# Attention tile: key and query factor spread over the outer products in place of the values, two product pairs summed on GpSimd

## The chip, the cores and the metric

The kernel runs on one core of a Trainium2 chip. The metric is the device time in microseconds of one execution, lower being better. Each time is that of a whole launch, so that constant loads at the start and the last store at the end count. In what follows PE is TensorE, DVE is VectorE, ACT is ScalarE, POOL is GpSimd and SP is SyncE, which here only issues DMAs.

## The reference, cut to what matters

All arithmetic is float32. The input is 4 sequences of 1024 tokens with 128 features. An attention layer, a feed-forward layer and a mixture with eight low-rank experts follow each other. The change is in the attention, with H = 16 heads of DH = 8 columns:

```
q = sigmoid(x @ Wq + bq); k = sigmoid(x @ Wk + bk); v = x @ Wv + bv
... (two rounds of running sums give sink_in, sink_alloc and src_comp, a factor per token and head)
qs = q * (sink_in / normal)[..., None]
vs = v * src_comp[..., None]
kv = jnp.cumsum(jnp.einsum('bhld,bhlm->bhldm', k, vs), axis=2)
x = jnp.einsum('bhld,bhldm->bhlm', qs, kv) * sink_alloc[..., None]
attn = x @ Wo + bo
```

For each token and head there is an outer product of 8 key columns d with 8 value columns m. It is summed along the tokens, and then contracted over d with the query factor. The projection by Wo follows.

## The kernel before, in words

The 4096 tokens are cut into 8 tiles of 512. A tile is held with the 128 features on the partitions (head times 8 plus column) and its tokens along the free axis. Odd tiles carry on the running sums of the even tile before them.

The instruction order of each engine is written out by hand. After an `opening` for tile 0 and a `second_step`, the function `step(s)` runs once per tile and works on four tiles at once: `a` = s+1 is in its attention denominators, `b` = s in its outer products, its output projection and its feed-forward layer, `c` = s-1 in the gate and the first half of the experts, `d` = s-2 in the second half of the experts. `closing` drains the last tiles. An engine takes its instructions strictly in this order. A wait on a semaphore holds all that stands behind it on the same engine, SP's queue of DMAs included.

The outer products go by value column m, in eight rounds:

1. `spread_vs(t, m)` on SP (L292) copies row m of each head of `vs` onto all 8 partitions of the head, from SBUF to SBUF, into `vb[:, m, :]`. It needs `vs`, which `values` (L1032) makes on DVE.
2. `outer_product(t, m)` on DVE (L1037) is `kv = k * vb[m]`: partition (h, d) holds column d of the key times value column m.
3. `cumulate_kv(t, m)` on DVE (L1043) is the running sum along the tokens. The first scan operand is a bank of ones in PSUM.
4. `product(t, m)` on POOL (L848) is `prod = cum_kv[m] * q_fac`. `prod` has four slots.
5. `reduce_out(t, m)` on PE (L404) multiplies the product, 128 tokens at a time, by `s_wor[:, m, :]`, a matrix in which row m of each head of Wo is repeated over the 8 partitions of the head. It sums over d and projects at once, in four matmuls (eight instruction records) of 128x128, into the PSUM bank `pO`.

The rounds 0 to 3 of tile `a` are begun at the end of a step, and the rounds 4 to 7 run at the beginning of the next step, where the tile has become `b`. `moments(b, 0)` on DVE waits for all eight `reduce_out`, and `inverse_std(b, 0)` on POOL for the moments.

The neighbours that the prediction speaks of are these. On POOL: `scaled_n2` (L874), `outer_residual` (L879), `inverse_std` (L835 to L841, four small instructions), `shifted_x` (L858), `constant_residual` (L886, writes `x2c`). On DVE: `second_relu` (L1141), `cumulate_q` and `cumulate_k` (L937), `k_times_cum_q` (L957, writes `kq`), `q_times_cum_k` (L964, writes `qk`). On PE: `expert_out` (L508), `project_v` (L340), and `head_sums` (L354), which takes `kq` and then `qk` and from which the denominators of the next tile come; further `hidden` (L421), `ffn_out` (L428), and `constant_row` (L517), done once, whose result `r_cmoe` DVE finishes.

## Time and profile before

| what | value |
|---|---|
| median of 3 runs | 418.44 us (418.27 to 419.03) |
| the profiled execution | 418.39 us, span 416.6 us |
| PE busy | 374.6 us, 90% |
| DVE busy | 327.9 us, 79% |
| POOL busy | 223.2 us, 54% |
| ACT busy | 216.6 us, 52% |
| DMA queue of SP | 25.96 MB, 24.5% of 16 engines |
| one step in the middle | 44.4 to 44.7 us |

The span goes from the first to the last instruction of the profiled execution. Its own time is 1.8 us longer. Busy times are those of the profile, and several engines work at the same time, so that they do not add up to the span.

### The profile page before, as it was taken

The numbers are of one execution on the slowest core, as the hardware profiler recorded it, in microseconds if no ns is written. First come the engines' busy times: TensorE is split into PE (matmuls) and PEld (weight loads), VectorE is DVE, ScalarE is ACT, GpSimd is POOL, SyncE is SP. The second block draws the span as 40 slices with busy tenths as digits, with TensorE's granted clock in tenths as the row PEclk, the third lists the DMA queues.
The fourth block names the chain that finished last, engine by engine and source line by source line (L and its number), as shares of the span: only waits on it lengthen the run. The fifth ranks groups of instructions, "written<-read, shape, count | busy, mean of one in ns | idle before, by whom it ended". The sixth has DMA issues, their size and how long they took to land.

```text
span 416.6 us, 6454 instructions
## 1 busy us (share of the span) xinstructions
PE 374.6 (90%) x2082; PEld 261.3 (63%) x2082; DVE 327.9 (79%) x787; ACT 216.6 (52%) x399; POOL 223.2 (54%) x263
## 2 busy tenths in 40 slices
PE   8897789788998999989998999899989997799991
PEld 3555556465756875677657774778478765775551
DVE  3649966599589988999799979997899889832632
ACT  2240226327853586538852795278644874175541
POOL 2017234983279527963497348942795369735211
PEclk9999999899999999999999999999999999999997
DMA  8236006400180007300560028000810063000000
GB/s 257 115 71 158 1 2 152 125 3 0 37 217 2 0 2 183 97 0 2 116 162 2 0 56 223 3 0 16 204 36 0 2 160 68 0 1 27 12 14 25
DMA packets 19857, 26.58 MB, mean 64 GB/s; under 512 B 1648, under 2 KB 9968, under 8 KB 19824
## 3 DMA queue, kind: packets, MB, share of 16 engines
q1 hardware_dynamic: 19680, 25.96, 24.5%
q8 instruction: 17, 0.28, 0.3%
q10 hardware_dynamic: 144, 0.21, 0.3%
q14 instruction: 16, 0.13, 0.1%
HBM read 7.29 MB, written 2.10 MB: 23 GB/s over the span
## 4 chain that ended last, share of the span: by engine, by line
PE 31%; DVE 27%; POOL 19%; issue 14%; DMA 5%; ACT 2%; SPq 0%; POOLq 0%; DVEq 0%; ACTq 0%
POOL prod L848 12%; PE pB L354 5%; DMA vb<-vs 5%; DVE kv L1037 5%; PE pY L428 4%; PE pG L421 3%; DVE cum_kv L1043 3%; DVE cum_ks L937 2%; PE pG L497 2%; POOL rstd L838 2%; PE pG L490 2%; DVE cum_q L937 2%; PE pY L508 2%; DVE cum_qs L937 2%; DVE gel L1141 2%
## 5 line engine op out<-in xcount | busy, mean ns | idle before, releaser
L848 POOL TENSOR_TENSOR prod<-cum_kv,q_fac 128x512 f32<-128x512 f32 x64 | 94.5, 1483 | 33.9 <-DVE cum_kv L1043 25.7
L404 PEld LDWEIGHTS pO<-s_wor,prod 128*128 128x128 f32 x512 | 62.2, 191 | 33.5 <-POOL prod L848 21.4
L404 PE MATMUL pO<-s_wor,prod 128*128 128x128 f32 x512 | 69.5, 281 | 14.0 <-POOL prod L848 13.9
L1037 DVE TENSOR_TENSOR kv<-k,vb 128x512 f32<-128x512 f32 x64 | 52.8, 825 | 6.7 <-DMA vb<-vs 6.7
L835 POOL TENSOR_TENSOR var_eps<-mv,s_con 128x4 f32<-128x4 f32 x32 | 9.9, 310 | 71.1 <-DVE mv L1063 71.1
L1043 DVE TENSOR_TENSOR_SCAN cum_kv<-p_ones,cum_kv,kv 128x512 f32<-128x512 f32 x32 | 40.5, 1275 | 0.6
L1043 DVE TENSOR_TENSOR_SCAN cum_kv<-p_ones,kv 128x512 f32<-128x512 f32 x32 | 38.5, 1213 | 0.5
L657 ACT ACTIVATE v<-pA,s_att 128x512 f32<-128x512 f32 x7 | 4.8, 687 | 62.9 <-PE pA L340 62.9
L754 ACT ACTIVATE relu<-pG,s_att 128x512 f32<-128x512 f32 x28 | 19.2, 684 | 27.4 <-PE pG L490 27.4
L508 PEld LDWEIGHTS pY<-s_moe,gel 128*128 128x128 f32 x256 | 30.7, 192 | 3.7 <-issue 1.9
L508 PE MATMUL pY<-s_moe,gel 128*128 128x128 f32 x256 | 32.6, 276 | 0.0
L838 POOL TENSOR_TENSOR rstd<-var_eps,s_con 128x4 f32<-128x4 f32 x32 | 32.5, 1014 | 0.0
L428 PE MATMUL pY<-s_ffn,gel 128*128 128x128 f32 x256 | 32.3, 276 | 0.0
L428 PEld LDWEIGHTS pY<-s_ffn,gel 128*128 128x128 f32 x256 | 30.4, 192 | 1.0 <-ACT pY L723 0.5
L421 PE MATMUL pG<-hT,s_ffn 128*128 128x512 f32 x64 | 30.5, 598 | 0.2
L484 PE MATMUL pG<-x2T,s_moe 128*128 128x512 f32 x60 | 30.6, 594 | 0.0
L490 PE MATMUL pG<-u1T,s_moe 128*128 128x512 f32 x60 | 30.5, 592 | 0.0
L497 PE MATMUL pG<-udT,s_moe 128*128 128x512 f32 x60 | 29.5, 605 | 0.0
L1141 DVE SCALAR_TENSOR_TENSOR gel<-pG,neg_bi,relu 128x512 f32<-128x512 f32 x28 | 20.3, 744 | 10.6 <-PE pG L497 10.5
L891 POOL TENSOR_TENSOR e_norm<-esrc,s_con 128x64 f32<-128x64 f32 x8 | 2.8, 346 | 40.8 <-ACT esrc L684 40.8
L354 PEld LDWEIGHTS pB<-s_att,kq 128*128 128x128 f32 x128 | 16.0, 191 | 12.5 <-issue 9.6
L712 ACT ACTIVATE gel<-pG,s_att 128x512 f32<-128x512 f32 x32 | 21.9, 685 | 2.8 <-PE pG L421 2.5
(164 smaller groups left out, 772.7 us busy)
## 6 DMA issues: line engine op xcount, KB each, us to landing
vb<-vs SPq DMA_DIRECT2D x64, 256.0 KB, 4.7
xT<-x_t SPq DMA_DIRECT2D x8, 256.0 KB, 4.3
xt<-x SPq DMA_DIRECT2D x8, 256.0 KB, 5.3
out<-y SPq DMA_DIRECT2D x8, 256.0 KB, 2.3
s_moe<-moe_w SPq DMA_DIRECT2D x1, 836.0 KB, 10.4
s_wor<-wo_rep SPq DMA_DIRECT2D x1, 512.0 KB, 8.2
s_ffn<-ffn_w SPq DMA_DIRECT2D x1, 512.0 KB, 8.9
s_con<-consts SPq DMA_DIRECT2D x1, 502.0 KB, 4.4
```

Source lines behind the costliest of these rows:

```text
L354: mm = pe.matmul(pB[:, end - P:end], src[:, s * P:(s + 1) * P], wide_sum, start=True, stop=True)
L404: mm = pe.matmul(pO3[:, s, :], prod[:, m % 4, s * P:(s + 1) * P], s_wor[:, m, :], start=False, stop=(m == DH - 1), skip_group_check=True)
L421: pe.matmul(pG[f % 2][:, :], w1[:, f * P:(f + 1) * P], hT[:, :], start=True, stop=True).then_inc(w1_done, 1)
L428: mm = pe.matmul(pY3[:, s, :], gel[:, f, s * P:(s + 1) * P], w2[:, f, :], start=False, stop=(f == FC - 1), skip_group_check=True)
L484: pe.matmul(expert_bank(t, f)[:, :], moe("wi")[:, f * P:(f + 1) * P], x2T[t.par][:, :], start=True, stop=False)
L490: pe.matmul(expert_bank(t, f)[:, :], moe("lb")[:, f * P:(f + 1) * P], u1T[:, :], start=False, stop=True).then_inc(in1_done, 1)
L497: pe.matmul(expert_bank(t, f)[:, :], moe("lb")[:, f * P:(f + 1) * P], udT[:, :], start=False, stop=True, skip_group_check=True).then_inc(i ...
L508: mm = pe.matmul(pY3[:, s, :], hsum[:, f, s * P:(s + 1) * P], wo[:, f, :], start=(f == 0 and s == 0), stop=(f == FC - 1), skip_group_check ...
L838: pool.tensor_tensor(rstd[i][:, :], var_eps[i][:, :], con("mhalf"), ALU.pow).then_inc(rstd_ready[i], 1)
L848: pool.tensor_tensor(prod[:, m % 4, :], cum_kv[t.par][:, m, :], q_fac[t.par][:, :], ALU.mult).then_inc(prod_ready, 1)
L1037: dve.tensor_tensor(kv[:, m % 3, :], k[t.par][:, :], vb[:, m, :], ALU.mult).then_inc(kv_ready, 1)
L1043: dve.tensor_tensor_scan(cum_kv[t.par][:, m, :], scan_ones, kv[:, m % 3, :], start, ALU.mult, ALU.add).then_inc(cumkv_ready, 1)
```

## The change

The outer products go by key column d instead of by value column m. Partition (h, m) now holds value column m, so that `vs` is used as it is. Row d of each head of `k` is spread by DMA into a ring of four slots `kb` (`spread_k`), and row d of each head of `q_fac` into `qb[:, d, :]` (`spread_q`). That makes 16 spreads of 256 KB a tile in place of 8. A product of one d is then a partial sum of the same output x, so that products can be added to each other before the projection, and all use the same Wo (`s_wo`, 64 KB in place of 512 KB). POOL adds products 0 and 1, and products 2 and 3 (`pair_sum`), so that PE does six `reduce_out` a tile in place of eight.

The orders change as well: the `reduce_out` of round 0 moves from the end of a step into the next, `expert_out(d, 0)` comes ahead of the later `reduce_out`, `factor_T` comes one `ffn_out` earlier, `query_factor` and the first round come ahead of `moments(b, 1)`, and `constant_row` moves from `opening` into `second_step`.

```
+PAIRS = 2
+SUMS = DH - PAIRS
...
-            def spread_vs(t, m):
-                sp.wait_ge(vs_ready, t.n + 1)
-                src = vs[m:P:DH, :].unsqueeze(1).to_broadcast([HEADS, DH, TOK])
-                sp.dma_start(vb[:, m, :], src).then_inc(vb_loaded[m], 16)
+            def spread_k(t, i):
+                sp.wait_ge(k_ready, t.n + 1)
+                wait(sp, kv_ready, DH * t.n + i - 3)
+                src = k[t.par][i:P:DH, :].unsqueeze(1).to_broadcast([HEADS, DH, TOK])
+                sp.dma_start(kb[:, i % 4, :], src).then_inc(kb_loaded[i], 16)
+            def spread_q(t, i):
+                sp.wait_ge(qfac_ready, t.n + 1)
+                wait(sp, prod_ready, DH * (t.n - 1) + i + 1)
+                src = q_fac[t.par][i:P:DH, :].unsqueeze(1).to_broadcast([HEADS, DH, TOK])
+                sp.dma_start(qb[:, i, :], src).then_inc(qb_loaded[i], 16)
...
-            sp.dma_start(s_wor[:, :, :], wo_rep).then_inc(y_free[0], 16)
+            sp.dma_start(s_wo[:, :], wo_att).then_inc(y_free[0], 16)
+            for i in range(4):
+                spread_k(Tile(0), i)
...
-                if B: spread_vs(b, 4); spread_vs(b, 5); spread_vs(b, 6)
                 if A and a.n == 2: load_xT(a)
+                if B: spread_k(b, 6); spread_k(b, 7)
+                if A and a.n >= 1:
+                    for i in range(4):
+                        spread_k(a, i)
                 if A and a.n >= 1: load_xt(a)
-                if B: spread_vs(b, 7)
                 if A and a.plus(1).exists() and a.n >= 2: load_xT(a.plus(1))
-                if A: spread_vs(a, 0); spread_vs(a, 1)
+                if A:
+                    for i in range(4):
+                        spread_q(a, i)
+                    spread_k(a, 4)
                 if D: store(d)
-                if A: spread_vs(a, 2); spread_vs(a, 3)
+                if A:
+                    for i in range(4, DH):
+                        spread_q(a, i)
+                    spread_k(a, 5)
...
+                if r < PAIRS:
+                    pe.wait_ge(pair_ready, PAIRS * t.n + r + 1)
+                    m = 2 * r
+                else:
+                    m = r + PAIRS
+                    pe.wait_ge(prod_ready, DH * t.n + m + 1)
...
-                if B: reduce_out(b, 1)
-                if A: project_k(a)
                 if D: inter2(d, 2); inter2(d, 3)
-                if B: reduce_out(b, 2)
+                if B: reduce_out(b, 0)
...
-                if B: reduce_out(b, 3); reduce_out(b, 4)
+                if D: expert_out(d, 0)
+                if B: reduce_out(b, 1)
                 if C: logits(c)
-                if B: reduce_out(b, 5); reduce_out(b, 6); reduce_out(b, 7)
-                if D: expert_out(d, 0)
+                if B: reduce_out(b, 2); reduce_out(b, 3); reduce_out(b, 4); reduce_out(b, 5)
                 if A: project_v(a); head_sums(a, 0, True); head_sums(a, 0, False)
...
-                if B: ffn_out(b, 2); ffn_out(b, 3)
+                if B: ffn_out(b, 2)
+                if A: factor_T(a)
+                if B: ffn_out(b, 3)
                 if C: u_T(c, False)
-                if A: factor_T(a)
...
-                if A: reduce_out(a, 0)
...
+            def pair_sum(t, r):
+                pool.wait_ge(prod_ready, DH * t.n + 2 * r + 2)
+                pool.tensor_tensor(prod[:, 2 * r, :], prod[:, 2 * r, :], prod[:, 2 * r + 1, :], ALU.add).then_inc(pair_ready, 1)
...
-                if B: product(b, 1); product(b, 2)
+                if B: product(b, 1); pair_sum(b, 0); product(b, 2)
                 if C: inverse_std(c, 2)
-                if B: product(b, 3); product(b, 4); product(b, 5); product(b, 6); product(b, 7); shifted_x(b)
+                if B: product(b, 3); pair_sum(b, 1); product(b, 4); product(b, 5); product(b, 6); product(b, 7); shifted_x(b)
...
-                dve.tensor_tensor(kv[:, m % 3, :], k[t.par][:, :], vb[:, m, :], ALU.mult).then_inc(kv_ready, 1)
+                dve.tensor_tensor(kv[:, m % 3, :], kb[:, m % 4, :], vs[:, :], ALU.mult).then_inc(kv_ready, 1)
...
+                if A: query_factor(a); outer_product(a, 0); cumulate_kv(a, 0)
                 if B: moments(b, 1)
-                if A: query_factor(a); outer_product(a, 0); cumulate_kv(a, 0)
```

In `product` the second factor becomes `qb[:, m, :]`, with a wait for its DMA, and in all waits `DH` on `red_ready` becomes `SUMS`.

## Rows read from the trace of the kernel before

**Rows 1.** The profile's page: granted clock of PE in 40 slices, in tenths.
```profile
PEclk9999999899999999999999999999999999999997
```
**Rows 2.** Busy time in stretches: us, PE, PEld, DVE, ACT, POOL (instructions), clock, DMA share.
```profile
222.90:267.60 44.70, 42.17 (x253) 31.06 (x253) 40.74 (x99) 27.23 (x50) 27.85 (x32) 1.00 0.27 66
...
252.30:272.20 19.90, 18.06 (x102) 12.59 (x102) 19.72 (x30) 6.51 (x12) 17.61 (x15) 1.00 0.35 91
...
238.08:252.33 14.25, 14.25 (x80) 10.07 (x81) 10.91 (x38) 12.08 (x27) 6.18 (x11) 1.00 0.35 81
```
**Rows 3.** Timeline of POOL, one middle step: start us, us, instruction, idle before.
```profile
253.97 1.60 POOL L879 TENSOR_TENSOR res<-res,x_b2n 128x512 f32<-128x512 f32 x1
255.71 3.05 POOL L848 TENSOR_TENSOR prod<-cum_kv,q_fac 128x512 f32<-128x512 f32 x2
258.72 0.65 POOL L835 TENSOR_TENSOR var_eps<-mv,s_con 128x4 f32<-128x4 f32 x1
...
267.80 1.27 POOL L848 TENSOR_TENSOR prod<-cum_kv,q_fac 128x512 f32<-128x512 f32 x1 [0.27 <-DVE cum_kv L1043]
...
270.25 1.27 POOL L886 TENSOR_TENSOR x2c<-x,c_gate 128x512 f32<-128x512 f32 x1
```
**Rows 4.** Timeline of DVE, the same step.
```profile
248.20 0.69 DVE L1037 TENSOR_TENSOR kv<-k,vb 128x512 f32<-128x512 f32 x1 [0.20 <-DMA vb<-vs]
...
253.00 1.43 DVE L1037 TENSOR_TENSOR kv<-k,vb 128x512 f32<-128x512 f32 x1
...
265.74 0.67 DVE L1037 TENSOR_TENSOR kv<-k,vb 128x512 f32<-128x512 f32 x1
...
271.17 0.91 DVE L957 SCALAR_TENSOR_TENSOR kq<-k,cum_q 128x512 f32<-128x512 f32 x1
...
272.10 0.67 DVE L964 SCALAR_TENSOR_TENSOR qk<-q,cum_k 128x512 f32<-128x512 f32 x1
```
**Rows 5.** Timeline of PE where a step meets the next one's denominators.
```profile
269.12 1.16 PE L404 MATMUL pO<-s_wor,prod 128*128 128x128 f32 x8 [0.38 <-POOL prod L848]
270.12 1.06 PE L508 MATMUL pY<-s_moe,gel 128*128 128x128 f32 x8
271.01 1.02 PE L340 MATMUL pA<-xT,s_att 128*128 128x512 f32 x2
272.22 1.13 PE L354 MATMUL pB<-s_att,kq 128*128 128x128 f32 x8 [0.19 <-DVE kq L957]
273.19 1.06 PE L354 MATMUL pB<-s_att,qk 128*128 128x128 f32 x8
```
**Rows 6.** SP's DMA issues in the same step.
```profile
249.31 4.46 SPq L292 DMA_DIRECT2D vb<-vs  x5
```
**Rows 7.** All instructions on tile vb: time of its DMAs to landing.
```profile
DMA to landing us min/median/max: 3.1/4.7/6.3
```
**Rows 8.** DVE and PE timelines of the opening.
```profile
29.46 0.69 DVE L1037 TENSOR_TENSOR kv<-k,vb 128x512 f32<-128x512 f32 x1 [2.69 <-DMA vb<-vs]
...
25.80 1.06 PE L517 MATMUL pM<-s_moe,bi_rep 128*128 128x128 f32 x8
```
**Rows 9.** Timelines of second_step and step 1: DVE, POOL, PE.
```profile
67.37 0.69 DVE L1037 TENSOR_TENSOR kv<-k,vb 128x512 f32<-128x512 f32 x1 [2.61 <-DMA vb<-vs]
...
78.14 1.26 POOL L879 TENSOR_TENSOR res<-res,x_b2n 128x512 f32<-128x512 f32 x1
...
67.85 3.73 PE L428 MATMUL pY<-s_ffn,gel 128*128 128x128 f32 x32
...
76.54 1.17 PE L404 MATMUL pO<-s_wor,prod 128*128 128x128 f32 x8 [2.38 <-POOL prod L848]
...
94.08 1.13 PE L354 MATMUL pB<-s_att,kq 128*128 128x128 f32 x8
```
**Rows 10.** POOL timeline of the last step.
```profile
343.07 1.59 POOL L879 TENSOR_TENSOR res<-res,x_b2n 128x512 f32<-128x512 f32 x1
...
356.89 1.27 POOL L848 TENSOR_TENSOR prod<-cum_kv,q_fac 128x512 f32<-128x512 f32 x1 [0.28 <-DVE cum_kv L1043]
```

More of the change, by code:

```diff
@@ L63, in run_steps, with build @@
         step(Tile(n))
-def build(nc, x, x_t, att_w, consts, wo_rep, rows, gate_row, ffn_w, moe_w, out):
+def build(nc, x, x_t, att_w, consts, wo_att, rows, gate_row, ffn_w, moe_w, out):
     ctx = ExitStack()
@@ L216, in build @@
         xt_loaded = [sem(f"xt_loaded{i}") for i in range(2)]
-        vb_loaded = [sem(f"vb_loaded{m}") for m in range(DH)]
+        kb_loaded = [sem(f"kb_loaded{d}") for d in range(DH)]
+        qb_loaded = [sem(f"qb_loaded{d}") for d in range(DH)]
         y_free = [sem(f"y_free{i}") for i in range(2)]
@@ L239, in build @@
         compT_ready, vs_ready = sem("compT_ready"), sem("vs_ready")
-        kv_ready, cumkv_ready, prod_ready, red_ready = (sem(n) for n in ("kv_ready", "cumkv_ready", "prod_ready", "red_ready"))
+        kv_ready, cumkv_ready, prod_ready, pair_ready, red_ready = (
+            sem(n) for n in ("kv_ready", "cumkv_ready", "prod_ready", "pair_ready", "red_ready"))
         res_ready = [sem(f"res_ready{i}") for i in range(4)]
@@ L396, in compensation_T, with reduce_out @@
                 spread_T(pB, comp_x[:, :, :].rearrange("p a b -> p (a b)"), compT_ready)
[L398 to L400 removed]
+            def reduce_out(t, r):
+                if r == 0:
                     pe.wait_ge(xseed_ready, t.n + 1)
[L402 removed]
+                if r < PAIRS:
[4 more added lines that the diff above has]
+                    pe.wait_ge(prod_ready, DH * t.n + m + 1)
                 for s in range(SUB):
[L404 to L405 removed]
+                    mm = pe.matmul(pO3[:, s, :], prod[:, m % 4, s * P:(s + 1) * P], s_wo[:, :],
+                                   start=False, stop=(r == SUMS - 1), skip_group_check=True)
                 mm.then_inc(red_ready, 1)
@@ L543, in opening @@
                 compensation_T(a); factor_T(a)
-                constant_row()
                 project_q(a.plus(1)); project_k(a.plus(1))
@@ L547, in opening @@
                 pe.wait_ge(y_free[0], 16)
-                reduce_out(a, 0)
             def second_step(b):
@@ L553, in second_step @@
                 keep_busy(2)
-                for m in range(1, 5):
-                    reduce_out(b, m)
+                reduce_out(b, 0); reduce_out(b, 1)
                 head_sums(a, 0, True); head_sums(a, 0, False); project_v(a)
                 keep_busy(1)
-                reduce_out(b, 5)
+                reduce_out(b, 2)
                 denominators_T(a, 0); denominators_T(a, 1)
                 keep_busy(1)
-                reduce_out(b, 6)
+                reduce_out(b, 3)
                 head_sums(a, 1, True)
@@ L565, in second_step @@
                 keep_busy(1)
-                reduce_out(b, 7)
+                reduce_out(b, 4); reduce_out(b, 5)
                 keep_busy(2)
@@ L572, in second_step @@
                     hidden(b, f)
+                constant_row()
                 for f in range(FC):
                     ffn_out(b, f)
-                keep_busy(3, pM)
-                reduce_out(a, 0)
+                keep_busy(3, pG[1])
             def closing(c):
@@ L843, in product @@
             def product(t, m):
-                if m == 0:
-                    pool.wait_ge(qfac_ready, t.n + 1)
+                pool.wait_ge(qb_loaded[m], 16 * (t.n + 1))
                 pool.wait_ge(cumkv_ready, DH * t.n + m + 1)
-                wait(pool, red_ready, DH * t.n + m - 3)
-                pool.tensor_tensor(prod[:, m % 4, :], cum_kv[t.par][:, m, :], q_fac[t.par][:, :], ALU.mult).then_inc(prod_ready, 1)
+                slot = m % 4
+                if m < 4:
+                    wait(pool, red_ready, SUMS * (t.n - 1) + (4 + slot) - PAIRS + 1)
+                elif slot < 2 * PAIRS:
+                    pool.wait_ge(red_ready, SUMS * t.n + slot // 2 + 1)
+                else:
+                    pool.wait_ge(red_ready, SUMS * t.n + slot - PAIRS + 1)
+                pool.tensor_tensor(prod[:, slot, :], cum_kv[t.par][:, m, :], qb[:, m, :], ALU.mult).then_inc(prod_ready, 1)
+            def pair_sum(t, r):
+                pool.wait_ge(prod_ready, DH * t.n + 2 * r + 2)
+                pool.tensor_tensor(prod[:, 2 * r, :], prod[:, 2 * r, :], prod[:, 2 * r + 1, :], ALU.add).then_inc(pair_ready, 1)
             def attention_input(t):
@@ L906, in second_step @@
                 a = b.plus(1)
-                for m in range(1, DH):
+                product(b, 1); pair_sum(b, 0); product(b, 2); product(b, 3); pair_sum(b, 1)
+                for m in range(4, DH):
                     product(b, m)
```

33 lines of the change are left out of this document (15 added, 18 removed).

## The prediction

> **What bounds the kernel now.** I read the table of stretches first, then the chain that ended last, then the timelines of the engines along that chain. A middle step takes 44.7 us and PE is busy for 42.2 of them, which looks like a kernel bound by PE [rows 2]. Two stretches of the step say more. From 238.08 to 252.33 PE is busy for 14.25 of 14.25 us: it runs hidden layers, transposes and expert products without a gap, and DVE waits for it. There is no output projection in this stretch [rows 2]. From 252.30 to 272.20 DVE is busy for 19.72 of 19.90 us and PE for 18.06, so that DVE sets the pace [rows 2]. DVE hands over to PE at 272.22, where `head_sums` has waited 0.19 us for `kq` [rows 5]. PE and DVE thus take turns in setting the step.
>
> A third party stands close behind. POOL makes its last product at 267.80 to 269.07 [rows 3]. PE then does the last `reduce_out` at 269.12, `expert_out(d, 0)` at 270.12, `project_v` at 271.01 and would be free for `head_sums` at 271.01 + 0.86 = 271.87 (its 1.02 us, less the 0.16 us by which each group overlaps the next: 269.12 + 1.16 against 270.12) [rows 5]. So the products could end only 0.35 us later before PE, and not `kq`, set the start at 272.22. POOL's 27.85 busy us of 44.70 [rows 2] hide this: in the stretch 252.30 to 272.20 it is busy for 17.61 of 19.90.
>
> One more thing is to be seen. The `kv` at 253.00 took 1.43 us where the one at 265.74 took 0.67, and it ended at 254.43 [rows 4]. On POOL, L879 was issued at 253.97 and lasted 1.60 us, though `x2c` of the same shape lasted 1.27 [rows 3]. Both engines read two SBUF tensors there, and each is stretched by the time in which the other has the memory. The same holds for `kq` at 271.17, 0.91 us [rows 4], beside `x2c`, which runs until 271.52 [rows 3], and for `var_eps`, 0.65 us [rows 3]. The Trainium skill (SBUF — State Buffer, "Who interferes with whom") says that a DVE instruction with two SBUF inputs and a reading GpSimd instruction exclude each other for the whole of one of them; the durations above agree. It speaks against this change. By this rule POOL's products end later, as summed below; without it, the nine instructions and `inverse_std` behind 255.57 would take 12.85 us and end at 268.4, before the present end.
>
> **The change, part by part.**
>
> *PE.* Two `reduce_out` a tile go, at 269.12 to 270.12 = 1.00 us each [rows 5], so 16 us of PE work in all. None lies in the stretch in which PE sets the pace, and in the other PE has gaps. Moving `expert_out(d, 0)` ahead takes 271.01 - 270.12 = 0.89 us from between the last `reduce_out` and `project_v` [rows 5]. This widens the slack of the last product from 0.35 to 1.24 us.
>
> *POOL.* Two additions of 512 columns a tile are added. An undisturbed POOL instruction of this shape takes 1.27 us, about 1.25 from start to start [rows 3]. They come between the products on which the end depends. I count the time in which DVE's and POOL's reads exclude each other, from the end of L879, 253.97 + 1.60 = 255.57. Before: seven products, 7 x 1.25 = 8.75; `inverse_std(c, 2)`, 1.6 (about 2.05 with its stall of 0.65 - 0.20 = 0.45); five `kv` of 0.6 (0.67 [rows 4] less the overlap with the next) = 3.0. The sum is 13.35, which gives 268.9, against 269.07 measured [rows 3]. So the count holds. After: nine instructions, 11.25, plus 1.6 and 3.0, less up to 0.6 where a `kv` slips under the tiny instructions of `inverse_std`: 15.25 to 15.85, ending at 270.8 to 271.4. I take 271.0. PE: 271.05 + 1.00 + 0.86 = 272.9 for `head_sums`, against 272.22. This is +0.7 us a step if nothing else is disturbed.
>
> *What is queued behind.* `shifted_x` and `x2c` stand behind the last product on POOL. Before, they ran under scans and PSUM reads of DVE and only `kq` met the end of `x2c`. Now they come at 271.0 to 273.5, just when DVE wants `kq` (271.2) and `qk`. If `kq` comes in ahead of `shifted_x`: `kq` to 271.6, `shifted_x` to 272.85, `qk` to 273.45, and the second half of `head_sums`, due at 272.9 + 0.97 = 273.87, does not wait: +0.7 us. If `shifted_x` comes in first: it ends at 272.25, `kq` 272.85, `x2c` 274.1, `qk` 274.7, and the second half starts at 274.75 instead of 273.19 [rows 5]: +1.6 us. Which comes first hangs on a tenth of a microsecond, and on the scans, which are a little longer in odd tiles. I take the middle, +1.2 us a step, and keep +0.7 and +1.6.
>
> *DVE.* It issues as many instructions as before. The wait for the spread of `vs`, 0.20 us in a middle step [rows 4], goes, but it lies before a wait for PE's stretch, so it gives nothing. `query_factor` moves ahead of `moments(b, 1)`; that delays `inverse_std(b, 1)` to about 251.0, just when ACT can use it: nothing.
>
> *Transfers.* Sixteen spreads a tile. SP issues five in 4.46 us, 0.89 each [rows 6], and a spread lands 3.1 to 6.3 us after its issue [rows 7]. `q_fac` is ready at about 246.3. Behind it stand q0 to q3, k4, a store, q4 to q7, k5: k5 is issued at 246.3 + 10 x 0.89 = 255.2 and lands at 258.3 to 261.5. DVE wants it at 261.6. q0 lands at about 249.5, and POOL wants it at 251. All is hidden, the last with little to spare by the upper bound. The spreads of k0 to k3 wait in the queue for the last `kv` of the step before (about 267) and are needed 25 us later. `load_xt` and `load_xT` behind them are late by some 15 us, and needed later still.
>
> *Start.* The first `kv` waits 2.69 us for its spread, the one of tile 1 2.61 us [rows 8, 9]. Both waits go, the second with the 0.6 us of `q_fac` under it. But kb4 of tile 0 stands fifth behind the q spreads and takes back about half of the first gain. Later, `moments(0, 1)` waits for `ffn_out`, which ends at 71.58 [rows 9] and into whose way `constant_row` comes, 1.06 - 0.16 = 0.9 us [rows 8]. With 1.5 us gained ahead of it I get -0.6 us at the end of L879, 79.40 [rows 9], so 78.8. DVE is ahead now and no longer paced by scans, so that four `kv`, `kq` and `qk` all fall among POOL's nine instructions: 78.8 + 11.25 + 1.6 + 1.8 (four `kv`, one under `inverse_std`) + 1.2 = 94.65. PE: + 1.9 = 96.55, against 94.08 [rows 9]. I take +2.4 us through step 1, with +0.7 (if half of the conflicts do not occur and the gain is 2) and +3.0 as bounds. PE had been idle for 2.38 us before 76.54 [rows 9], and the slice from 72.9 to 83.3 shows 0.8 of the full clock [rows 1]; `load_xT(2)` now stands behind ten spreads, so this gap gets longer and more slow matmuls follow. The deadline that they would miss is POOL's, much later: nothing.
>
> *Last step.* L879 ends at 344.66 [rows 10]. + 11.25 + 1.6 + 3.0 - 0.6 = 359.9, against 358.16 [rows 10]. The moments, the feed-forward layer and the experts of the last tile all follow from this: +1.8 us (1.3 to 2.4).
>
> *Sum.* +2.4 + 5 x 1.2 (steps 2 to 6) + 1.8 = +10.2 us on the profiled execution's 418.39 us, so 428.6. It stands 0.05 us from the median of the runs, 418.44. The forecast's own range is +0.7 + 3.5 + 1.3 = 5.5 to +3.0 + 8.0 + 2.4 = 13.4: 423.9 to 431.8.
>
> **The rivals.**
>
> *PE is what bounds the step.* For it: 42.2 busy us of 44.7. Then 16 projections of 0.89 to 1.00 us come off: 402 to 404 us. Against it: the projections lie where PE waits. It decides only if the products end before 270.3 and DVE gets shorter too. Chance 0.07.
>
> *The additions are hidden.* POOL is busy for only 54% of the span. If the additions and the reads of DVE lie beside each other, the products end before 270.3 and nothing is lost in the steps. The start gives -0.6 to -1.5, the end costs 0 to +1.8: 417 to 420.2, I say 418.4. Against it is the count above, which meets the present end within 0.2 us. Chance 0.13.
>
> *The spreads come late.* If 256 KB take more than 0.9 us when thirteen go in one burst, say 1.3, k5 lands at 246.3 + 13 + 3.1 = 262.4 and DVE stands for 0.8 us more a step: 428.6 + 6 x 0.8 = 433. Chance 0.10.
>
> *The products end late, as summed.* 428.6. Chance 0.66. The remaining 0.04 is for a fall of the clock in the middle steps, which would give over 434.
>
> **How the numbers follow.** The first rival is faster. The second is faster, the same and slower in about equal parts (0.05, 0.04, 0.04). All else is slower. A difference of 0.2%, 0.8 us, is about what runs of this kernel can tell. So faster 0.12, same 0.04, slower 0.84. The range leaves out the first rival, two thirds of the second and the clock: 419.0 to 433.5.
>
> **What would show it.** Right, if a middle step lasts about 45.8 us; if POOL runs from the end of L879 to the last product without a gap; if `kv`, `kq` or `qk` last 1.0 to 1.9 us more often than before; if `head_sums` on `kq` starts straight behind `project_v`; and if PE's idle time is named by POOL. The count is wrong if the last product of a middle step ends less than 1.3 us later after L879 than now. The transfers are wrong if DVE's idle time names kb or POOL's names qb in the middle steps. The forecast falls if DVE's scans, and not the products, still come last before `head_sums`.

## The result and the profile after

The changed kernel takes 439.28 us (median; 438.22 to 439.61), the one before, in the same session, 418.36 us (418.25 to 419.03): 1.0488 times as long, 95% interval 1.047 to 1.0506. Slower was forecast, 428.6 us with a range to 433.5; it is 10.7 us slower than that. The profiled execution has a span of 437.7 us against 416.6. Two of the runs below had a disturbed execution, far longer at a lower clock (538.72 us in e14_spreads, 741.31 us in e16_fewer): the ratios leave these out, and as that of e14_spreads was the profiled one, nothing is read from its trace.

I cut both traces at `rden` (L969 before, L1000 after), of which DVE computes one a tile. The last two columns split a middle step (steps 2 to 6, mean) at L879, which is L909 after: from `rden` to its start, and from its end to the next `rden`. These cuts serve for all experiments below; a step is named by the tile whose `rden` begins it.

| us | `rden` of tile 2 at | five middle steps | last `rden` to end | to L909 | behind L909 |
|---|---|---|---|---|---|
| before | 96.14 | 222.48 | 98.0 | 24.37 | 18.53 |
| after | 99.68 | 236.44 | 101.6 | 25.72 | 19.92 |
| measured | +3.5 | +14.0 (2.8 each) | +3.6 | +1.35 | +1.39 |
| predicted | +2.4 | +6.0 (1.2 each) | +1.8 | 0 | +1.2 |

So a middle step loses as much ahead of the products as behind them, and the prediction had put nothing ahead. What a middle step lost beyond the forecast lies ahead of L909. The granted clock of PE on the page of after, beside [rows 1]:

```profile
PEclk9997999698996999899988999899979997799997
```

It falls in every step: in stretches of 1 us the lower of PE's two levels (1.2 GHz of 2.4) holds for 3.4 to 10.2 us of each of the five middle steps, and for none of them before. The table of stretches for one middle step of after, that of tile 5 as in [rows 2] (columns as there):

```profile
241.20:288.99 47.79, 41.97 (x239) 30.94 (x238) 42.42 (x99) 27.31 (x50) 30.96 (x34) 0.96 0.45 105
```

PE is busy for 41.97 us of a step that is 3 us longer, and POOL has 3.1 us more. The timeline of POOL in that step, beside [rows 3]:

```profile
262.31 0.56 POOL L856 TENSOR_TENSOR var_eps<-mv,s_con 128x4 f32<-128x4 f32 x1 [2.48 <-DVE mv L1096]
...
267.68 1.67 POOL L909 TENSOR_TENSOR res<-res,x_b2n 128x512 f32<-128x512 f32 x1
269.31 1.27 POOL L874 TENSOR_TENSOR prod<-cum_kv,qb 128x512 f32<-128x512 f32 x1
270.66 1.71 POOL L878 TENSOR_TENSOR prod<-prod 128x512 f32<-128x512 f32 x1
272.33 1.26 POOL L874 TENSOR_TENSOR prod<-cum_kv,qb 128x512 f32<-128x512 f32 x1
...
275.02 0.20 POOL L862 TENSOR_TENSOR shift<-neg_mean,rstd 128x4 f32<-128x4 f32 x1
275.18 1.71 POOL L874 TENSOR_TENSOR prod<-cum_kv,qb 128x512 f32<-128x512 f32 x1
276.96 1.83 POOL L878 TENSOR_TENSOR prod<-prod 128x512 f32<-128x512 f32 x1
278.75 5.39 POOL L874 TENSOR_TENSOR prod<-cum_kv,qb 128x512 f32<-128x512 f32 x4
```

Nine products and sums run from 269.35 to 284.14 almost without a gap, 14.79 us against 13.5 before (14.55 to 15.03 in the five middle steps, against 13.19 to 13.50). The count had said 15.25 to 15.85. The additions last 1.7 to 1.8 us, and `shift` of `inverse_std(c, 2)`, behind the first of them, is done at 275.22. What PE does meanwhile, beside [rows 5]:

```profile
272.51 1.13 PE L431 MATMUL pO<-s_wo,prod 128*128 128x128 f32 x8 [0.52 <-POOL prod L878]
276.96 0.66 PE L463 MATMUL pM<-s_con,x 128*128 128x128 f32 x4 [3.31 <-ACT x L722]
277.45 1.64 PE L535 MATMUL pY<-s_moe,gel 128*128 128x128 f32 x8
278.88 2.03 PE L431 MATMUL pO<-s_wo,prod 128*128 128x128 f32 x8
280.71 1.28 PE L470 MATMUL pM<-s_moe,x2T 128*128 128x128 f32 x8
281.82 3.74 PE L431 MATMUL pO<-s_wo,prod 128*128 128x128 f32 x32
285.40 1.02 PE L362 MATMUL pA<-xT,s_att 128*128 128x512 f32 x2
286.26 1.05 PE L376 MATMUL pB<-s_att,kq 128*128 128x128 f32 x8
287.74 1.16 PE L376 MATMUL pB<-s_att,qk 128*128 128x128 f32 x8 [0.42 <-DVE qk L995]
```

PE has nothing to do for 3.31 us, until ACT has normalised with that `shift`. Then a `reduce_out` takes 2.03 us instead of 1.16 [rows 5]: PE runs at the lower level from 277.8 to 281.1, 3.4 us. The last four `reduce_out` follow without a gap, and `project_v` begins at 285.40, 0.2 us later than POOL's last product would allow (284.14 + 0.05 + 1.00). PE had 0.35 us of slack there before.

The gap ahead of `x2_T` has three parts, and the addition is the smallest. In the step of tile 4, counted from `rden`, PE is done with the work ahead of it at 31.18 us instead of 32.31, as one `reduce_out` (0.89 to 1.00 us by [rows 5]) of the step now stands ahead of `x2_T` and two did before. ACT's result comes at 34.49 instead of 32.80: 0.98 us of that is the later end of L909, 0.71 the addition ahead of `inverse_std(c, 2)`. So the gap grows from 0.49 to 3.31 us.

DVE in the same stretch, beside [rows 4]:

```profile
275.05 0.71 DVE L1070 TENSOR_TENSOR kv<-kb,vs 128x512 f32<-128x512 f32 x1 [1.43 <-DMA kb<-k]
...
278.90 1.67 DVE L1070 TENSOR_TENSOR kv<-kb,vs 128x512 f32<-128x512 f32 x1
...
286.03 1.66 DVE L995 SCALAR_TENSOR_TENSOR qk<-q,cum_k 128x512 f32<-128x512 f32 x1
```

DVE waits for the spread of k5, which the forecast had hidden, and all behind it is late by that, down to `qk`. `qk` is stretched beside `x2c` and ends at 287.69; the second half of `head_sums` has waited 0.42 us for it. So DVE, PE and POOL come late to the same place, each for a reason of its own. SP's issues of the step show DVE's reason, beside [rows 6]:

```profile
259.14 3.29 SPq L304 DMA_DIRECT2D qb<-q_fac  x4
262.52 1.31 SPq L297 DMA_DIRECT2D kb<-k  x1
263.88 1.28 SPq L308 DMA_DIRECT2D out<-y  x1
265.25 4.41 SPq L304 DMA_DIRECT2D qb<-q_fac  x4
269.79 11.38 SPq L297 DMA_DIRECT2D kb<-k  x7
```

Ten issues from 259.14 to 269.79 are 1.07 us each, not 0.89, and k5 lands 5.2 us later, at 275.0. All instructions on kb, beside [rows 7] (the first row has ns, shortest, median and longest, of an issue):

```profile
L297 SPq DMA_DIRECT2D kb<-k x64: 529/1264/1354, 7.4 to 366.4; - x64
...
  DVE kv L1070: 10.9, 7
...
DMA to landing us min/median/max: 3.0/4.9/6.0
```

DVE waited for kb seven times, 10.9 us in all: 2.39 us in the opening and 0.97 to 1.73 us in each of six steps.

### The profile page after: what moved, and what is told of

Read it like the earlier page. It is cut to its first block, busy times and chain, and to the rows that moved or that the text cites. A ratio compares the mean times of both kernels' runs of the same rounds, so it can differ in the third digit from the quotient of the medians.

```text
span 437.7 us, 6407 instructions
## 1 busy us (share of the span) xinstructions
PE 375.4 (86%) x1954; PEld 264.7 (60%) x1954; DVE 333.1 (76%) x787; ACT 217.2 (50%) x399; POOL 244.4 (56%) x279
## 2 busy tenths in 40 slices
DMA packets 29074, 42.90 MB, mean 98 GB/s; under 512 B 2672, under 2 KB 11120, under 8 KB 29040
## 4 chain that ended last, share of the span: by engine, by line
PE 38%; DVE 23%; issue 10%; SPq 10%; POOL 10%; DMA 6%; ACT 3%; POOLq 0%; DVEq 0%; ACTq 0%
SPq L304 7%; DMA kb<-k 6%; PE pY L455 6%; PE pB L376 6%; POOL prod L874 5%; PE pG L448 4%; DVE kv L1070 4%; PE pO L431 4%; PE pY L535 3%; DVE cum_kv L1076 2%; DVE cum_ks L968 2%; PE pG L524 2%; PE pA L382 2%; DVE qk L995 2%; PE pG L517 2%
## 5 line engine op out<-in xcount | busy, mean ns | idle before, releaser
L874 POOL TENSOR_TENSOR prod<-cum_kv,qb 128x512 f32<-128x512 f32 x64 | 85.5, 1346 | 21.9 <-DVE cum_kv L1076 8.3
L431 PE MATMUL pO<-s_wo,prod 128*128 128x128 f32 x384 | 54.7, 299 | 10.2 <-POOL prod L878 9.4
L431 PEld LDWEIGHTS pO<-s_wo,prod 128*128 128x128 f32 x384 | 51.5, 213 | 18.6 <-issue 12.4
L1070 DVE TENSOR_TENSOR kv<-kb,vs 128x512 f32<-128x512 f32 x64 | 52.6, 824 | 10.9 <-DMA kb<-k 10.9
L535 PEld LDWEIGHTS pY<-s_moe,gel 128*128 128x128 f32 x256 | 35.5, 216 | 3.7 <-issue 1.9
L535 PE MATMUL pY<-s_moe,gel 128*128 128x128 f32 x256 | 37.6, 302 | 0.0
L455 PE MATMUL pY<-s_ffn,gel 128*128 128x128 f32 x256 | 33.3, 276 | 0.0
L878 POOL TENSOR_TENSOR prod<-prod 128x512 f32<-128x512 f32 x16 | 26.3, 1645 | 1.3
L722 ACT ACTIVATE x<-res,shift,rstd 128x128 f32<-128x128 f32 x32 | 13.2, 483 | 27.8 <-POOL shift L862 27.8
```

The lines of the kernel that those rows point to most:

```text
L431: mm = pe.matmul(pO3[:, s, :], prod[:, m % 4, s * P:(s + 1) * P], s_wo[:, :], start=False, stop=(r == SUMS - 1), skip_group_check=True)
L455: mm = pe.matmul(pY3[:, s, :], gel[:, f, s * P:(s + 1) * P], w2[:, f, :], start=False, stop=(f == FC - 1), skip_group_check=True)
L535: mm = pe.matmul(pY3[:, s, :], hsum[:, f, s * P:(s + 1) * P], wo[:, f, :], start=(f == 0 and s == 0), stop=(f == FC - 1), skip_group_check ...
L874: pool.tensor_tensor(prod[:, slot, :], cum_kv[t.par][:, m, :], qb[:, m, :], ALU.mult).then_inc(prod_ready, 1)
L1070: dve.tensor_tensor(kv[:, m % 3, :], kb[:, m % 4, :], vs[:, :], ALU.mult).then_inc(kv_ready, 1)
```

## The experiments

Each was timed in three rounds beside the kernel before, which took 418.4 to 419.2 us in each session. The ratios are to it, with their 95% intervals.

**e1_kfirst: the late k5 mended.** On SP's queue:

```diff
-                if B: spread_k(b, 6); spread_k(b, 7)
...
-                    spread_k(a, 4)
+                    spread_k(a, 4); spread_k(a, 5); spread_q(a, 4); spread_k(a, 6); spread_k(a, 7)
                 if D: store(d)
                 if A:
-                    for i in range(4, DH):
+                    for i in range(5, DH):
                         spread_q(a, i)
-                    spread_k(a, 5)
```

> The changed kernel with the last four key spreads of a tile brought forward in SP's queue: k5 directly behind k4, k6 and k7 ahead of the store and of q5 to q7. In the trace of the changed kernel DVE waits 1.4 to 1.7 us a step for k5. If late spreads carry a good part of the loss, DVE no longer waits and the time falls by 6 to 10 us, to about 430 to 433. If POOL's additions set the end of the products alone, DVE gains nothing by arriving earlier and the time stays at 438 to 440.

443.65 us (1.0585, 1.0557 to 1.0612). The waits for kb fall from 10.9 to 2.4 us, and the kernel gets slower. PE's wait ahead of `x2_T` becomes longer (this view: who waited for whom, us, times, longest):

```profile
PE pM L461 <- ACT x L720: 24.6, 6, 4.3
```

Of the 5.2 us by which this trace is longer than that of the changed kernel, only 1.3 lie in the five middle steps; 1.8 lie ahead of `rden` of tile 2 and 2.2 in the last step. Early spreads gain nothing as long as PE's gap is there.

**e2_keep: the clock mended.** Four matmuls whose result is overwritten fill the gap:

```diff
+                if B and s.n >= 2: keep_busy(4, pM)
                 if C: x2_T(c)
```

> The changed kernel with four filler matmuls of 512 columns (about 3.4 us) on PE ahead of the transpose of x2 in each step, where PE now idles for 3.3 us and then shows a lower granted clock for some 7 us. If the fallen clock costs time on the path, the granted clock is back at 0.99 and the time falls by 1 to 2 us a step, to 426 to 433. If the slow matmuls are hidden behind POOL and the late spreads, the time stays at 438 to 440. If the filler itself gets in the way, it is over 441.

438.09 us (1.0447, 1.0421 to 1.0473). The clock's row has 9 from step 2 to near the end, but only 1.2 us come back, with k5 still late (kb 10.7 us).

**e5_kfirst_keep: both.**

> The changed kernel with both edits at once: the last key spreads brought forward, and four filler matmuls ahead of the transpose of x2. Alone, the first moved the time from 439.3 to 443.7 and the second to 438.1. In the trace of the first, DVE no longer waits for k5, but PE idles 4.3 us before the transpose of x2, falls to half its clock, and its late projections hold back POOL's product 6 and the next head_sums. If each fault hid behind the other, the two edits together give 1.5 to 2.5 us a step: 425 to 431. If they are independent, or neither is on the path, 438 to 443.

432.85 us (1.033, 1.0313 to 1.0347). Alone the two give +4.4 and -1.2 us, together -6.4. Against e1 the filling gives 10.8 us. In the step of tile 4 `x2_T` starts 35.3 us behind `rden` in e1 and in e5 alike, so the filling does not end the gap sooner; what it changes is the speed of the matmuls behind it: 6.8 us at the lower level in each of e1's middle steps, 3.4 in one of e5's. The stretch behind L909 is 18.70 us, within 0.2 of before, with both additions in it. Late spreads and slow matmuls cover each other: each mended alone leaves the other in place.

**e3_nopairs and e6_kfirst_nopairs: no additions.** PE does all eight projections again; e6 has the queue of e1 too.

```diff
-PAIRS = 2
+PAIRS = 0
...
             def pair_sum(t, r):
+                if r >= PAIRS: return
```

> The changed kernel with PAIRS = 0: no additions on POOL, eight output projections a tile. If the additions (2.5 us of POOL and their exclusion of DVE's reads) are the cause, as predicted, the time falls by about 8 to 12 us, to 427 to 431. If late spreads and the clock are the cause, it falls by less than 4 us, to 435 to 439, since k5 is as late as before.

> The changed kernel with the key spreads brought forward and no additions on POOL. If additions and late spreads each give a loss of their own and overlap in the changed kernel (additions alone on the kernel before cost 15.5 us; no additions alone gained nothing), then taking away both gives 420 to 428. If the new form of the outer products costs by itself in some third way, it stays above 432.

438.86 us (1.0494, 1.0445 to 1.0543) and 439.51 us (1.0506, 1.0452 to 1.056). Taking the additions out of the changed kernel gives nothing; with early spreads it gives 4.1 us (e6 against e1). PE's wait ahead of `x2_T` is still 17.9 us in e3, 2.68 to 2.80 us a middle step, so the additions alone do not make it. Nor does such a gap always bring the clock down. In two of the five middle steps of e3, those of tiles 4 and 5, it stays up:

```profile
275.02 0.66 PE L463 MATMUL pM<-s_con,x 128*128 128x128 f32 x4 [2.73 <-ACT x L722]
```

These two steps last 45.97 and 47.39 us, against 44.33 and 44.75 before. The new layout thus loses 1.6 and 2.6 us a step with neither additions nor a lower clock, 0.9 and 2.0 of it ahead of L909. In other steps POOL now waits for PE's projections, for up to 3.07 us, so these runs do not take the additions away and leave all else.

**e7_kfirst_inv: `inverse_std(c, 2)` ahead of the addition.** With the queue of e1; on PE `expert_out(d, 0)` and then `x2_T` also go ahead of `reduce_out(b, 0)`.

```diff
-                if B: product(b, 1); pair_sum(b, 0); product(b, 2)
+                if B: product(b, 1)
                 if C: inverse_std(c, 2)
+                if B: pair_sum(b, 0); product(b, 2)
```

> The changed kernel with the key spreads brought forward and inverse_std(c, 2) on POOL moved from behind product 2 to behind product 1, ahead of the addition; on PE the transpose of x2 goes ahead of the first reduce_out. The idle time of PE and its fallen clock come from the late x2. If the order on POOL makes them, PE no longer idles 3 to 4 us, the clock stays near 0.99 and the time is 425 to 432. If the exclusion between POOL's and DVE's reads alone sets the step, it stays at 434 to 443.

439.42 us (1.0488, 1.0472 to 1.0503). That is no better than the changed kernel, but 4.2 us better than e1, from which it differs in this order alone. The wait ahead of `x2_T` shrinks from 24.6 to 11.1 us over the run. `reduce_out(b, 0)` behind it then waits for the sum, 2.54 us in a middle step, and the clock still falls in three of the five, where it falls in all five of e1. Part of the gap only moves.

**e4_adds and e9_memset: the additions alone, in the kernel before.** POOL adds the same pairs into a tile that nothing reads, or writes 1344 columns there with a memset:

```diff
+            def extra_sum(t, r):
+                pool.wait_ge(prod_ready, DH * t.n + 2 * r + 2)
+                wait(pool, extra_ready, 2 * t.n + r)
+                pool.tensor_tensor(extra[:, :], prod[:, 2 * r, :], prod[:, 2 * r + 1, :], ALU.add).then_inc(extra_ready, 1)
...
-                if B: product(b, 1); product(b, 2)
+                if B: product(b, 1); extra_sum(b, 0); product(b, 2)
...
-                if B: product(b, 3); product(b, 4); product(b, 5); product(b, 6); product(b, 7); shifted_x(b)
+                if B: product(b, 3); extra_sum(b, 1); product(b, 4); product(b, 5); product(b, 6); product(b, 7); shifted_x(b)
```

> The kernel before with the two additions on POOL at the same places, written to a tile that nobody reads; the eight output projections stay as they were, so that the sum is work added for nothing. The count of the prediction gives +1.2 us or more in the middle steps and +1.8 at the end: 426 to 430, more if expert_out is still behind the last projection. If the additions are hidden where no spread is late, the time is 418 to 421.

> The kernel before with two memsets of 1344 columns a tile on POOL in the places where e4_adds had its two additions, about 1.3 us each: the same time on POOL, but nothing is read from SBUF. If POOL's time alone counts, the time is that of e4_adds, 433 to 436. If the exclusion of DVE's reads carries part of it, kv, kq and qk are stretched no more than in the kernel before and the time is 422 to 431.

434.54 us (1.0373, 1.0341 to 1.0404) and 425.7 us (1.0171, 1.0137 to 1.0204). The additions alone cost 15.5 us: 1.44 a middle step, all of it behind L909 (19.96 us), 5.5 us through step 1, and 3.5 in the last step. The lower clock is not what the middle steps pay for: the three in which it never falls (tiles 2, 4 and 6) last 45.91 us, against 44.32 to 44.34 before, and the other two 45.90 and 46.07, against 44.74 and 44.75. Ahead of tile 2 it matters: e17 below is the same kernel up to there, has 3.4 us at the lower level instead of 10.3, and is there at 99.61 us instead of 101.62, 3.5 us behind the kernel before. The memset lasts 1.22 us and the addition 1.46 on the mean, yet the memset costs 6.6 us of the 15.5. In the step of e4 whose products begin at 265.53, POOL shows:

```profile
271.60 0.47 POOL L843 TENSOR_TENSOR shift<-neg_mean,rstd 128x4 f32<-128x4 f32 x1
272.02 1.26 POOL L851 TENSOR_TENSOR prod<-cum_kv,q_fac 128x512 f32<-128x512 f32 x1
273.36 1.67 POOL L856 TENSOR_TENSOR extra<-prod 128x512 f32<-128x512 f32 x1
```

The addition has an undisturbed time of 1.27 us (it shows at 267.23 in that step) and 1.67 beside a `kv`.

**e12_adds_keep and e15_before_keep: the filling in the kernel before,** with and without the additions of e4; the edit is that of e2.

> The kernel before with the two extra additions on POOL (434.5 us) and four filling matmuls ahead of x2_T. If part of the 15.5 us that the additions cost there is a fall of the clock, the filling brings it to 429 to 431 us, the summed +10 to +12. If they cost by POOL's and DVE's order alone, it stays at 434 to 436 us.

> The control of the filling: the kernel before with the four filling matmuls ahead of x2_T. PE has no long gap there before, so the filling can only cost: 3.6 us of PE work a step, of which some lies in front of x2_T and the projections. 419 to 424 us. If it comes out at 418 or below, the filling helps by itself and the runs with it are to be read with that.

432.48 us (1.0335, 1.0317 to 1.0352) and 422.28 us (1.0084, 1.0066 to 1.0102). The filling is no free cure: it costs 3.4 us by itself. The stretch behind L909 is 19.93 us in e12, 19.96 in e4 and 19.22 in e15. The additions lengthen it by 1.4 us without the filling and by 0.7 with it. The clock is not the difference, since e4's steps at full clock are as long as its others; the 0.7 us that the filling costs alone is hidden beside the additions. What the filling does mend is the last step: from the last `rden` to the end 99.4 us against 101.5 in e4 and 98.0 before.

**e14_spreads: the transfers alone.** Eight more spreads of `q_fac` a tile into a tile that nothing reads, behind `load_xT`:

```diff
+                if B:
+                    for i in range(8):
+                        extra_spread(b, i)
                 if A: spread_vs(a, 0); spread_vs(a, 1)
```

> The kernel before with eight extra spreads of the query factor a tile into a tile that nothing reads, issued behind load_xT, where no spread of the values waits behind them. If the new layout's doubled traffic costs by itself (other transfers land late, SBUF is disturbed), 421 us or more. If a transfer costs only where somebody waits for it, 418 to 419 us.

418.78 us (0.9996, 0.9987 to 1.0006). This traffic costs nothing measurable where nothing waits behind it. It does not test the long bursts of the changed kernel, in which an issue took 1.04 to 1.07 us.

**e16_fewer and e17_adds_fewer: less PE work.** In the kernel before, without and with the additions of e4, three quarters of two output projections are left out from tile 2 on, so the output lacks that part:

```diff
-                for s in range(SUB):
+                for s in range(SUB if m not in (1, 3) or t.n < 2 else 1):
```

> The kernel before with three quarters of the output projection of products 1 and 3 left out from tile 2 on: 1.5 us of PE work less a step and nothing on any other engine. If the projections lie where PE waits anyway, as the prediction has it, 417.5 to 418.5 us. If PE bounds the step, 410 us. If less work lets the clock fall, 420 us or more and lower digits in the clock's row.

> The kernel before with the two extra additions on POOL (434.5 us) and three quarters of the projections of products 1 and 3 left out from tile 2 on. If the two savings and costs are separate, 433 to 434.5 us. If the fewer projections together with the late products let PE idle long enough for its clock to fall, 436 to 440 us, which is the whole of the change without any of its new transfers.

419.35 us (1.0016, 1.0002 to 1.0029) and 441.25 us (1.0542, 1.0515 to 1.0569). This is the sharpest pair. 1.5 us less PE work a step changes next to nothing where POOL is on time, and adds 6.7 us where the additions make it late (e4, 434.54). PE in e17:

```profile
276.29 0.66 PE L438 MATMUL pM<-s_con,x 128*128 128x128 f32 x4 [2.41 <-ACT x L702]
276.78 0.39 PE L406 MATMUL pO<-s_wor,prod 128*128 128x128 f32 x2
278.79 2.08 PE L406 MATMUL pO<-s_wor,prod 128*128 128x128 f32 x8 [1.62 <-POOL prod L851]
280.66 1.91 PE L445 MATMUL pM<-s_moe,x2T 128*128 128x128 f32 x8
```

Two gaps, and matmuls at half speed behind them: 6.8 us at the lower level in every middle step, where e4 has 3.4 us in two of the five. The stretch behind L909 grows to 21.33 us. With the old layout, transfers and queue this kernel is as slow as the changed one, but in another place: the changed one has 25.72 us ahead of L909 and 19.92 behind it, this one 24.65 and 21.33.

**e10_kfirst_nopairs_keep, e11_epref, e13_all: the rest of the new layout.** e10 is e5 without additions. e11 is e5 with an order changed on DVE and one on SP. e13 is e11 without additions.

```diff
-                if C: gate(c, 12); masked_lora(c, True)
+                if C: gate(c, 12)
                 if A: prefix_e(a)
+                if C: masked_lora(c, True)
...
-                if A and a.n == 2: load_xT(a)
...
                 if A and a.n >= 1: load_xt(a)
+                if A and a.n == 1: load_xT(a.plus(1))
```

> The new layout without the two pair additions (PE does all eight projections), with k5 to k7 issued directly behind k4, and with four filling matmuls ahead of x2_T from step 2 on. If late spreads, clock and additions are the only three costs, this is the kernel before with other transfers: steps of 44.5 to 45.0 us and 418 to 422 us. If the products are also limited by PE's projections (POOL waited 2.9 us a step for PE without the additions), or if the longer queue of spreads costs on its own, steps stay at 45.8 or above and the time is 428 to 434 us.

> k5 to k7 early and four filling matmuls (432.85 us as they stand) and two orders more: the scan e_pref stands on DVE ahead of the masked LoRA product, so that it starts before POOL's x_bo instead of behind it, and the load of xT(2) stands ahead of the queue of q spreads. If the 1.0 us that odd tiles lose between the denominators and the third GELU is e_pref's wait for x_bo, steps with an odd tile get 1 us shorter (46.07 to about 45.6 a step on average) and step 1 gets 1 us shorter for xT(2): about 429.5 us. If DVE's order there does not matter, 432 to 433 us.

> No additions, k5 to k7 early, filling matmuls, e_pref ahead of the masked LoRA product, xT(2) ahead of the q spreads. If the layout itself is free, this has everything mended and comes within 3 us of the kernel before, possibly 1 to 2 us below it, since two waits of 2.6 us for a spread are gone in its first 70 us: 416 to 421 us. If the layout costs by something else, 426 us or more.

e10 takes 436.0 us (1.0419, 1.0395 to 1.0443), e11 431.02 us (1.0295, 1.0279 to 1.031) and e13 430.96 us (1.0314, 1.0264 to 1.0364). The order of `e_pref` matters in e11: tile 5, which had 26.47 us ahead of L909, has 25.40. The order of xT(2) does not show: step 1 waits 8.4 us for it in e5 and not at all in e11, yet `rden` of tile 2 comes at 99.93 and 100.16. Without the additions the middle steps are 0.3 us (e10 against e5) and 0.5 us (e13 against e11) shorter each, but `rden` of tile 2 is 4.0 and 2.4 us later, so that e13 is no faster than e11 and e10 is slower than e5. But even with everything mended and no additions the stretch ahead of L909 is 25.32 us, 0.95 over before. That cost is not the additions': in e4 and e17 the stretch is 24.38 and 24.65.

**e18_mended and e19_moments: DVE's order undone,** in e11 and in the changed kernel:

```diff
-                if A: query_factor(a); outer_product(a, 0); cumulate_kv(a, 0)
                 if B: moments(b, 1)
+                if A: query_factor(a); outer_product(a, 0); cumulate_kv(a, 0)
```

> The kernel with k5 to k7 early, filling matmuls, e_pref and xT(2) moved (431.0 us), and one order more put back as it was before the change: on DVE, moments(b, 1) stands ahead of query_factor(a) and the first outer product. In that kernel the stretch from a step's rden to the start of L909 lasts 25.50 us on average against 24.37 before, and the stretch from the end of L909 to the next rden 18.70 against 18.53. If the first stretch is long because inverse_std(b, 1) waits for moments that stand behind q_fac, kv and a scan, it falls to 24.4 and the time by six times 1.1, to 424 to 425.5 us, with both additions still in it. If that order is neutral, as the prediction has it, 430 to 432 us.

> The changed kernel (439.3 us) with this one order put back and nothing else. If the order costs 1 us a step on its own, 432 to 434 us, unless q_fac, which now comes 1 to 2 us later, makes the late k5 later still and gives it back: then 436 to 440 us. If the order is neutral, 439 to 441 us.

434.17 us (1.0359, 1.0342 to 1.0377) and 441.18 us (1.0534, 1.0514 to 1.0553). Both get slower, by 3 and 2 us. Yet the stretch ahead of L909 does what was expected: 25.50 to 24.67 us in e18, 25.72 to 24.90 in e19. The stretch behind it takes more than that back: 18.70 to 19.94 us in e18. DVE shows how, first e11 with its last three `kv` and `qk`, then e18 with its two long `kv` (the first stands just ahead of L908) and `qk`:

```profile
269.04 0.67 DVE L1069 TENSOR_TENSOR kv<-kb,vs 128x512 f32<-128x512 f32 x1
270.94 0.67 DVE L1069 TENSOR_TENSOR kv<-kb,vs 128x512 f32<-128x512 f32 x1
272.84 0.67 DVE L1069 TENSOR_TENSOR kv<-kb,vs 128x512 f32<-128x512 f32 x1
...
278.97 1.65 DVE L994 SCALAR_TENSOR_TENSOR qk<-q,cum_k 128x512 f32<-128x512 f32 x1
```

```profile
263.63 1.76 DVE L1069 TENSOR_TENSOR kv<-kb,vs 128x512 f32<-128x512 f32 x1
...
276.27 1.67 DVE L1069 TENSOR_TENSOR kv<-kb,vs 128x512 f32<-128x512 f32 x1
...
283.41 1.66 DVE L994 SCALAR_TENSOR_TENSOR qk<-q,cum_k 128x512 f32<-128x512 f32 x1
```

`qk` is long in both. But no `kv` of e11's middle steps lasts over 0.74 us, while each of e18's has one of 1.68 to 1.76 and one of 1.67 to 1.73. The late L909 lets `kv` fall between POOL's instructions instead of beside them, and the undone order brings the collisions back, which e4 has too. In e18 and e19 POOL also waits for qb, 18.4 us in seven waits, but ahead of L909, in the stretch that got shorter. So the costs of the additions and of the new order are no sum. Both stretches together take 42.90 us before, 44.20 in e11, 44.61 in e18 and 44.34 in e4: a step pays the one or the other, 1.3 to 1.7 us. This reading fits the four kernels; no run tests it by itself. The changed kernel, with 45.64, has late spreads and clock on top.

## Why the prediction was wrong

**Direction: right. The additions: right in the old layout, and by luck in the new one.** The count of POOL's instructions foretold +1.2 us a step (+0.7 to +1.6) and +2.4 us through step 1. Alone, in the old layout, the additions cost 1.44 a step (e4) and at least 3.5 through step 1. The nine instructions took 14.55 to 15.03 us in the middle steps, not the 15.4 counted, since fewer of DVE's reads fell beside them. The stretch behind L909 of the changed kernel, +1.39 us, seems to confirm the +1.2. It does not: with early spreads and the filling (e5, e11) the products end as late, and the stretch is only 0.17 us longer than before, with both additions in it. The prediction had itself found that the slack of the last product grows to 1.24 us; most of the delay goes into that. The +1.39 is late spreads and clock, and without the additions the changed kernel is as slow (e3).

What failed are three terms that the prediction put at nothing.

**The step that failed: "PE. ... None lies in the stretch in which PE sets the pace", together with the chance of 0.04 for a fall of the clock.** I priced two projections less at nothing, and so they nearly are (e16: 1.0016), but only while the other engines are on time. PE waits 3.31 us ahead of `x2_T` where it waited about 0.5 in a middle step before: 1.1 us of the growth is the `reduce_out` that no longer stands ahead of it, 1.0 the later L909, 0.7 the addition. Behind the gap it runs at half speed, and its slack ahead of `head_sums` is gone. The price is 10.8 us where no spread is late (e1 against e5), and 1.2 us where they are (e2). e17 shows that additions and less PE work cost 22.4 us in the old layout without any new transfer. That is what the pair can do; as the loss lies elsewhere in the step, it does not show that the changed kernel's loss is this one. I had seen such a gap with slow matmuls in step 1 [rows 9, 1] and called the deadline POOL's, without asking what `inverse_std(c, 2)`, which stands behind the first addition, holds up.

**"Transfers. ... All is hidden": failed.** Counted from `rden`, k5 was issued at 28.6 us in the step shown and not at 25.7. The ten issues took 10.65 us instead of 8.9, and `q_fac` was ready 1.1 us later than forecast. The second holds for this step and, with 0.9 us, that of tile 2; in those of tiles 3, 4 and 6 `q_fac` was on time (16.7 to 16.8 us), k5 was issued at 27.3 to 27.5, and DVE waited 1.21 to 1.73 us all the same, since it was ready at 31.0 to 31.3. So the term that was mis-sized is the issue, 1.04 to 1.07 us each in the burst instead of 0.89. The spread landed after 5.2 us, within [rows 7]. My rival "the spreads come late" had the mechanism and a wait of 0.8 us, with a chance of 0.10. Its price shows only with the clock kept: 438.09 against 432.85 us, 5.2 us. Eight more spreads where nobody waits cost nothing (e14).

**"`query_factor` moves ahead of `moments(b, 1)` ... nothing": failed as a term.** The step is 0.83 us longer ahead of L909 by it (e11 against e18; 0.82 in the changed kernel against e19), most of the 1.35 us that the forecast had at nothing. Its net cost is not positive, though, since undoing it loses 3 us (2 us in e19).

**Not foreseen:** in the step of tile 5 `e_pref` falls behind POOL's `x_bo` and lasts 1.31 us instead of 0.31, about 1 us in that step; in the other middle steps it lasts 0.31 to 0.32. The instruction ahead of it on DVE starts 0.24 us later there than before; why is open. So are some 0.3 us of the 1.35.

**Start and end: mis-sized.** The start was +3.5 instead of +2.4. Step 1 waits 6.3 us for xT(2), behind ten spreads. That delay was named and priced at nothing, and this much was right as far as e11 shows it. The gain in the opening did not come: kb4 is waited for, 2.39 us, and the first product 5.97 us for qb. What sets the start is open; it is no earlier without the additions (100.12 in e3). The end was +3.6 instead of +1.8. In the old layout the additions' order accounts for +1.4 there (e12, clock kept), which is in the range given, and the clock in the last step for the other 2.1 (e4 against e12). In the new one the filling alone did not bring the end back (101.7 in e2), with early spreads it did (100.2 in e5).

**The account.** With k5 early, the clock kept, `e_pref` and xT(2) in order (e11, span 429.7) 13.1 us of the 21.1 stay: 4.0 to tile 2, 6.6 in the middle steps, 2.4 at the end, some of which is the filling's own work. 8.0 us came back, 6.4 of the median by spreads and filling. Of what stays in the middle steps 1.13 us each lies ahead of L909 and 0.17 behind it; no run splits it between the additions and the orders, since each takes over when the other is mended. No version of the new layout that was tried comes near the kernel before.

## What to carry to other kernels

When work is added to an engine, look at every small instruction queued behind it, not only at the result that it delays. Here `inverse_std`, 1.7 us of tiny instructions, feeds an engine that then stands for 3 us and comes back at half speed. Look also at what stood ahead of the wait on that engine: a projection moved away from there widened the gap more than the addition did. Work taken off a waiting engine is free only while its gaps stay short; price the two edits of such a change together, in one kernel, since each alone told 1.037 and 1.002 and both together 1.054. And when two causes cover each other, mending one proves nothing: mend both, then take one away.

## What the runs showed of the hardware

- PE's idle 3.31 us is followed by 3.4 us at half speed (eight matmuls of 128x128 in 2.03 us instead of 1.05 to 1.16), and so is one of 1.97 us in e4 (1.95 for eight). One of 2.73 us in e3 is not. The filling matmuls, 3.60 us, kept full speed in the five middle steps of e2.
- The issue of a spread of 256 KB takes 0.53 to 1.50 us of SP in the changed kernel, 1.26 at the median for kb and 1.04 for qb. Eight more spreads a tile cost nothing (0.9996) when nobody waits for them.
- A POOL addition of 128x512 lasts 1.27 us alone and up to 1.83 beside DVE's reads; a `kv` 0.67 alone and up to 1.76. A POOL memset in the place of each addition lasts 1.22 us every time.
